# Two graph convolutions: the sums of all blocks kept in PSUM, one-hots made from SBUF operands

## The chip, the cores and the metric

The program runs on one NeuronCore of a Trainium2 chip, as one launch. The metric is the device time of that launch in microseconds (us). Before the change it is 5357.61 us, the median of three runs (5348.63 to 5358.73).

## The reference

The whole is a two-layer network over a graph of 6250 nodes (256 features) and 100,000 edges, sorted by destination. The change touches only the second layer's graph part and the mixing part that runs beside it. The graph part is two graph convolutions, one after the other:

```
h   = x @ W                                  # to 64 columns
msg = h[src] * (dinv[src] * dinv[dst])
agg = segment_sum(msg, dst) + h * dinv**2    # 6250 x 64
out = relu(agg + b)
```

The second one is computed as its sum first and its product with W2 (64 to 256 columns) afterwards, so both sum rows of 64 columns. The mixing part needs, over all nodes, the sum of `v^T k` per pair of 128 columns and the sum of `k` (k and v are layer-normalised per head of 32), and after that, for each node, `gelu(x_n @ M + c) @ w2 + b2 + x_n`.

## The kernel before

Nodes are cut into NB = 49 blocks of 128, edges into NT = 782 tiles of 128. Since the edges are sorted, a tile lies in one block or in a few neighbouring ones; each pair (tile, block) is a *step*. With the steps that are split at block borders and padding there are 832 steps, in NG = 104 groups of GS = 8. Tables made earlier on the chip say for each step which block it belongs to (`btab`), in which slot of a ring its tile lies (`stab`), and for each group how many groups of tiles must have landed (`need`).

`convolve(nc, m, a, which)` runs twice, for which = 0 and 1. Five engines work at once, each with its own program:

- GpSimd (L1850 to L1861) issues one indirect DMA for each tile (L1857): 128 rows of 64 floats, gathered from the table `t_d` in HBM by the row numbers in `m.srct` (SBUF), into one of 96 ring slots (12 groups). Ahead of a group g it waits until group g-2 has landed, and counts it in `tiles_in` (L1853, L1854); and it waits until the step groups that could still read the slots are summed (`summed` >= g-4, L1856). Its program is written out in full, it has no loop.
- VectorE makes for each step group eight one-hots of 128 x 128 (`one_hot`, L1924): is_equal between `iota`, a copy in PSUM made at the start (L1905), and the local destinations `m.dl` in SBUF.
- TensorE (`total`, L2073 to L2082) multiplies each one-hot with its tile's rows into 64 columns of PSUM bank 0 or 1.
- VectorE adds these 64 columns into the block's row of `m.agg` in SBUF (`add`, L1926 to L1936), one instruction for each step, each waiting for the one before (`added`). `m.agg` starts as a copy of the node's own table (L1906).
- Beside this, for which = 0, TensorE projects each block to keys and values (`project`, L2089), VectorE adds the bias (`add_bias`, L1965) and scales (`scale`, L1954, L1958), ACT squares, and `sum_kv` (L2099, L2101) accumulates the sums in banks 4 to 7. For which = 1 `up` (L2111), ACT's gelu (L2057) and `down` (L2120) run the mixing network in banks 2 and 3. SyncE loads the block of transposed rows that they need (`load`, L1894), after the one before is used (`mixed`).

The order on each engine is written out by `pipeline`: in iteration k VectorE does one_hot(2k), add(2k-1), variance(k-1), one_hot(2k+1), add(2k), scale(k-1), add_bias(k). TensorE does total(2k), sum_kv(k-2), project(k), total(2k+1). After 52 iterations `refresh` (L1993 to L2000) scales, adds the bias, clips and scales again, in seven chunks of seven blocks, and SyncE stores the new table. A stage ends with a barrier of all engines. The convolutions stand between `combine_and_project` and `finish_and_route1`. The scoring stage of the first layer (`score_edges`) is of the same kind: 832 indirect DMAs from GpSimd (L653) beside VectorE's L692, L700 and L705.

Of the kernel before, what the change touches and what calls it, by code (L numbers as in the profile page):

```python
# [1805 lines left out]
def convolve(nc, m, a, which):  # L1806
# [4 lines left out]
    with ExitStack() as ctx:  # L1811
# [5 lines left out]
        oh = sb("oh", [P, 2, GS, P])  # L1817
        xt = sb("xt", [P, D])
        bank = [ctx.enter_context(nc.psum_tensor(f"v{which}_bank{i}", [P, 512], F32)) for i in range(8)]
        s = {n: m.sem(f"v{which}_" + n) for n in "in0 in1 tiles_in oh_ready summed added started xt_in weights".split()}  # L1820
        landed = [s["in0"], s["in1"]]
        iota = bank[3 + which][:, 0:P]
        table = m.t_d.rearrange("b p n -> (b p) n")
        if which == 0:
# [5 lines left out]
            b1row = sb("b1row", [P, MH])  # L1830
            s.update({n: m.sem("v0_" + n) for n in ("chain centred kv_made kvb_ready squared summed16 var_ready std_ready rstd_ready "
                                                    "kn_ready kv_used scaled biased table stored sums_out").split()})
            mixed = s["kv_made"]
        else:
# [7 lines left out]
            t_ps, m2_ps = (bank[i][:, :].rearrange("p (c d) -> p c d", c=KC) for i in (5, 6))  # L1842
            s.update({n: m.sem("v1_" + n) for n in ("ht_made ht_ready out_made xn_ready xb_ready mixed res_ready "
                                                    "fold_in chain kvt t_made t_back m2_made folded").split()})
            mixed = s["ht_made"]

        with nc.Block() as block:
            @block.gpsimd
            def _(pool):
                for g in range(TG):  # L1850
                    if g >= 2:
                        pool.wait_ge(landed[g % 2], 16 * GS * (g // 2))
                        pool.sem_inc(s["tiles_in"], 1)  # L1853
                    if g + NB // GS + 2 > RING // GS:  # L1854
                        pool.wait_ge(s["summed"], g + NB // GS + 2 - RING // GS)
                    for t in range(g * GS, min((g + 1) * GS, NT)):  # L1856
                        nc.gpsimd.indirect_dma_start(rows[:, t % RING, :], None, table,  # L1857
                                                     bass.IndirectOffsetOnAxis(ap=m.srct[:, t:t + 1], axis=0)).then_inc(landed[g % 2], 16)
                for g in (TG - 2, TG - 1):
                    pool.wait_ge(landed[g % 2], 16 * (GS * (g // 2) + min(GS, NT - g * GS)))  # L1860
                    pool.sem_inc(s["tiles_in"], 1)  # L1861

            @block.sync
            def _(sp):
# [26 lines left out]
                def load(k, u, r):  # L1891
                    if at_least(k, 1):
                        sp.wait_ge(mixed, k)
                    sp.dma_start(xt[:, :], block_rows(m.xnt_d, k)).then_inc(s["xt_in"], 16)  # L1894
                pipeline(sp, NB, 1, (0, load))
                if which == 0:
                    for c in range(NB // 7):
                        sp.wait_ge(s["table"], c + 1)
                        sp.dma_start(m.t_d[7 * c:7 * c + 7].rearrange("b p n -> p b n"), m.table[:, 7 * c:7 * c + 7, :]).then_inc(s["stored"], 16)
                    sp.wait_ge(s["stored"], 16 * (NB // 7))  # L1900

            @block.vector
            def _(dve):
                V = nc.vector
                V.tensor_copy(iota, m.iota[:, :]).then_inc(s["started"], 1)  # L1905
                V.tensor_copy(m.agg[:, :, :], m.table[:, :, :]).then_inc(s["started"], 1)  # L1906
                dve.wait_ge(s["started"], 2)
# [13 lines left out]
                def one_hot(g, u):  # L1921
                    if at_least(g, 2):
                        dve.wait_ge(s["summed"], g - 1)
                    V.tensor_tensor(oh[:, u, :, :], iota.unsqueeze(1).to_broadcast([P, GS, P]),  # L1924
                                    m.dl[:, bass.ds(g * GS, GS)].unsqueeze(2).to_broadcast([P, GS, P]),
                                    ALU.is_equal).then_inc(s["oh_ready"], 1)  # L1926

                def add(g, u):
                    dve.wait_ge(s["summed"], g + 1)
                    blocks = blocks_of(nc, m, mybir.EngineType.DVE, g * GS, GS)  # L1930
                    for k in range(GS):
                        t = g * GS + k
                        if at_least(t, 1):
                            dve.wait_ge(s["added"], t)
                        V.tensor_tensor(of_block(m.agg, blocks[k]), of_block(m.agg, blocks[k]), bank[u][:, k * MH:(k + 1) * MH],  # L1935
                                        ALU.add).then_inc(s["added"], 1)  # L1936
# [24 lines left out]
                def add_bias(k, u, r):  # L1961
# [3 lines left out]
                    V.tensor_tensor(kvb[:, :, :, :].rearrange("p t h d -> p (t h d)"), bank[2][:, :],  # L1965
# [10 lines left out]
                def finish(k, u, r):  # L1976
                    dve.wait_ge(s["xb_ready"], k + 1)
                    dve.wait_ge(s["out_made"], k + 1)
                    V.tensor_tensor(xb[:, :], xb[:, :], bank[3][:, 0:D], ALU.add).then_inc(s["mixed"], 1)
# [5 lines left out]
                def refresh():  # L1985

                    dve.wait_ge(s["added"], NS)
                    part = lambda t, c: t[:, 7 * c:7 * c + 7, :]
                    dinv = lambda c: m.dinv[:, 7 * c:7 * c + 7].unsqueeze(2).to_broadcast([P, 7, MH])
                    n = NB // 7  # L1990
                    for c in range(n + 2):
                        if c < n:
                            V.tensor_tensor(part(m.agg, c), part(m.agg, c), dinv(c), ALU.mult).then_inc(s["scaled"], 1)  # L1993
                        if 0 <= c - 1 < n:
                            dve.wait_ge(s["scaled"], c)
                            V.tensor_tensor(part(m.agg, c - 1), part(m.agg, c - 1), b1row[:, :].unsqueeze(1).to_broadcast([P, 7, MH]),
# [6 lines left out]
                def fold():  # L2003
# [9 lines left out]
                    for q in range(KC):  # L2013
# [12 lines left out]
                    V.tensor_tensor(m.c2[:, :], b1[:, :], bank[7][:, 0:KC], ALU.add).then_inc(s["folded"], 1)  # L2026

                conv = ((0, lambda k, u, r: one_hot(2 * k, 0)), (1, lambda k, u, r: add(2 * k + 1, 1)),
                        (0, lambda k, u, r: one_hot(2 * k + 1, 1)), (0, lambda k, u, r: add(2 * k, 0)))
                if which == 0:  # L2030
                    pipeline(dve, NR, 1, conv[0], conv[1], (1, variance, NB), conv[2], conv[3], (1, scale, NB), (0, add_bias, NB))
                    refresh()
                else:
                    fold()
                    dve.wait_ge(s["weights"], 32)
                    pipeline(dve, NR, 1, conv[0], conv[1], (1, normalise, NB), conv[2], conv[3], (1, finish, NB))

            @block.scalar
            def _(act):
# [12 lines left out]
                def gelu(k, u, r):  # L2052
# [3 lines left out]
                    for q in range(KC):  # L2056
                        last = nc.scalar.activation(ht[:, q, :], bank[2][:, q * P:(q + 1) * P], ACT.Gelu, bias=m.c2[:, q:q + 1])  # L2057
                    last.then_inc(s["ht_ready"], 1)
                if which == 0:
                    pipeline(act, NB, 1, (1, root), (0, square))  # L2060
                    act.wait_ge(s["kv_used"], NB)
                    for q in range(KC):
                        nc.scalar.copy(m.gram[:, q, 0:P + 1], bank[4 + q][:, 0:P + 1]).then_inc(s["sums_out"], 1)
                        nc.scalar.copy(m.gram[:, q, P + 1:2 * P + 1], bank[6 + q][:, 0:P]).then_inc(s["sums_out"], 1)
                    act.wait_ge(s["sums_out"], 2 * KC)
                else:
                    act.wait_ge(s["folded"], 2)
                    pipeline(act, NB, 1, (0, gelu))

            @block.tensor  # L2070
            def _(pe):
                def total(g, u):
                    pe.wait_ge(s["oh_ready"], g + 1)  # L2073
                    if at_least(g, 2):
                        pe.wait_ge(s["added"], GS * (g - 1))
                    tiles = tiles_needed(nc, m, mybir.EngineType.PE, g)
                    at = slots_of(nc, m, mybir.EngineType.PE, g * GS, GS)
                    pe.wait_ge(s["tiles_in"], tiles)
                    for k in range(GS):
                        last = nc.tensor.matmul(bank[u][:, k * MH:(k + 1) * MH], oh[:, u, k, :], of_block(rows, at[k]),  # L2080
                                                start=True, stop=True)
                    last.then_inc(s["summed"], 1)  # L2082

                def project(k, u, r):
# [3 lines left out]
                    for q in range(KC):  # L2088
                        last = nc.tensor.matmul(bank[2][:, :], xt[:, q * P:(q + 1) * P],  # L2089
# [3 lines left out]
                def sum_kv(k, u, r):  # L2093
                    rows_ = LAST if isinstance(k, int) and k == NB - 1 else P
                    first, final = isinstance(k, int) and k == 0, isinstance(k, int) and k == NB - 1
# [640 lines left out]
```

## Time and profile before

| What | Value |
|---|---|
| Timed runs | 5357.61 us median (5348.63 to 5358.73) |
| Profiled execution, first to last instruction | 5935.3 us |
| Window of convolution 0 | 2878 to 4045 us, then its end to 4088 us |
| Window of convolution 1 | 4089 to 5280 us |
| Gathers (L1857), both convolutions | 1564, 1483.7 us busy, 949 ns each |
| GpSimd idle before them | 957.2 us |
| Adds (L1935) | 1664, 366.5 us busy |
| One-hots (L1924) | 208, 253.7 us busy, 1220 ns each |
| Matmuls of the steps (L2080) | 3328 rows, 716.2 us busy |
| Gathers of the scoring stage (L653) | 832, 859.8 us busy, 1033 ns each |

The profiled execution is another one than the timed ones, and no time of it is recorded other than its span. An fp32 matmul stands in the rows as two passes, each with its load of weights. A row names line, engine, operation, and the tiles as out<-in; 128x1024 is partitions x elements. "Idle before" is the time in which that engine did nothing ahead of such a row, and the name behind the arrow is what ended it. The releaser is inferred from a semaphore's number; numbers are used again by later stages, so a name can be that of an earlier stage. "issue" is time in which the engine waited for nothing that the profile shows. The table of times and the page are read together: first the length of a stage, then which engine's row of instructions fills it.

### The profile page before, as it was taken

To read this page: it belongs to the slowest core of one execution; us is meant where nothing else is said; L and a number is where in the kernel's file an instruction comes from. 1 tells how busy PE (TensorE), PEld (TensorE's weight loads), DVE (VectorE), ACT (ScalarE), POOL (GpSimd) and SP (SyncE) were. 2 spreads that over 40 slices of the span, in tenths; PEclk is the share of its full clock that TensorE was granted. 3 is DMA by queue.
4 is the path that set the end of the run, shared out by engine and by line. 5 is a ranking of instruction groups with operands and counts; after the bars stand their busy time and mean duration, and the time that the engine had idled before them with its cause. 6 is when DMAs were issued, how large, how long until landed. Compare 5 with 4: busy or idle time off the path is not lost. (4 is left out here: it accounts for less than half of the span.)

```text
span 5935.3 us, 66919 instructions
## 1 busy us (share of the span) xinstructions
PE 3546.3 (60%) x13782; PEld 2710.2 (46%) x13783; DVE 2982.8 (50%) x6982; ACT 1018.9 (17%) x2146; POOL 3055.9 (51%) x2888
## 2 busy tenths in 40 slices
PE   4744455454389865998444544454445454466998
PEld 3633233232267654776433433333434444455666
DVE  5466566666899964445433333334333333354443
ACT  0111121121179801221000000000000000013121
POOL 1266677676368624221466666663666666612111
PEclk9877767776599976998566566655555555566999
DMA  4487666666578762223311111111111111123221
GB/s 108 136 217 211 202 207 203 204 206 195 158 227 271 224 188 88 63 63 97 106 28 28 29 28 28 29 29 32 28 29 28 28 29 28 29 62 98 70 87 37
DMA packets 432122, 617.01 MB, mean 104 GB/s; under 512 B 100329, under 2 KB 309161, under 8 KB 431721
## 3 DMA queue, kind: packets, MB, share of 16 engines
q1 hardware_dynamic: 304733, 389.03, 21.1%
q0 software_dynamic: 107440, 200.97, 14.1%
q10 hardware_dynamic: 19852, 25.94, 1.6%
q8 instruction: 33, 0.54, 0.0%
q14 instruction: 64, 0.52, 0.0%
HBM read 419.67 MB, written 209.64 MB: 106 GB/s over the span
## 5 line engine op out<-in xcount | busy, mean ns | idle before, releaser
L1857 POOL DMA_INDIRECT big<-t_d,src_tiles x1564 | 1483.7, 949 | 957.2 <-issue 450.8
L2080 PE MATMUL v_bank<-big,v_oh 128*128 x3328 | 716.2, 390 | 1216.6 <-issue 830.3
L2080 PEld LDWEIGHTS v_bank<-big,v_oh 128*128 128x128 f32 x3328 | 674.7, 300 | 1302.8 <-issue 1302.2
L653 POOL DMA_INDIRECT big<-xl_d,src_steps x832 | 859.8, 1033 | 378.1 <-issue 356.0
L1935 DVE TENSOR_TENSOR big<-big,v_bank 128x64 f32 x1664 | 366.5, 220 | 1285.3 <-DMA xj_d<-big 973.2
L759 PE MATMUL se_z_ps<-big,se_oht 128*128 x1664 | 608.7, 517 | 628.5 <-issue 385.9
L759 PEld LDWEIGHTS se_z_ps<-big,se_oht 128*128 128x128 f32 x1664 | 386.8, 250 | 850.4 <-issue 780.7
L692 DVE TENSOR_TENSOR se_z<-se_z_ps,big 128x528 f32<-128x528 f32 x416 | 291.4, 700 | 461.1 <-DMA es_ts<-src_p 256.8
L1122 PE MATMUL ae_bank<-ae_v,ae_oh 128*128 128x266 f32 x1664 | 402.3, 397 | 49.8 <-DVE big L1106 36.7
L1081 POOL TENSOR_TENSOR ae_v<-ae_v,ex 128x1792 f32<-128x1792 f32 x104 | 334.1, 3215 | 178.1 <-DMA ae_v<-xj_d 178.0
L1122 PEld LDWEIGHTS ae_bank<-ae_v,ae_oh 128*128 128x128 f32 x1664 | 310.4, 191 | 141.5 <-DVE big L1106 53.0
L1106 DVE TENSOR_TENSOR big<-big,ae_bank 128x266 f32 x832 | 303.8, 425 | 13.2 <-PE ae_bank L1122 7.5
L1924 DVE TENSOR_TENSOR v_oh<-v_bank,dl_steps 128x1024 f32<-128x1024 f32 x208 | 253.7, 1220 | 92.5 <-issue 92.0
L729 ACT ACTIVATE se_oht<-se_dlb,se_place 128x1024 f32<-128x1024 bf16 x104 | 119.4, 1148 | 986.6 <-DMA es_ts<-src_p 498.3
L700 DVE SCALAR_TENSOR_TENSOR se_w<-se_z,se_attb 128x512 f32<-128x512 f32 x416 | 284.8, 685 | 0.1
L1599 POOL DMA_INDIRECT y_d<-e_y,e_idx x106 | 104.1, 982 | 348.1 <-DVE e_idx L1562 328.6
L705 DVE TENSOR_REDUCE ex<-se_w 128x512 f32 (+1 forms) x416 | 281.6, 677 | 0.0
L2526 POOL DMA_INDIRECT out<-e_y,e_idx x64 | 63.0, 984 | 422.3 <-DVE e_y L2569 407.6
L1069 ACT ACTIVATE ae_oh<-iota,dl_steps 128x128 f32<-128x128 f32 x832 | 254.5, 388 | 60.0 <-PE ae_bank L1122 51.7
L2622 PE MATMUL e_bank<-big,e_ht 128*128 128x256 f32 x1024 | 225.3, 381 | 0.7 <-issue 0.7
L2611 PE MATMUL e_bank<-e_xt,big 128*128 128x465 f32 (+1 forms) x512 | 214.4, 577 | 1.6 <-DVE e_xt L2545 1.6
L2057 ACT ACTIVATE v_ht<-v_bank,c 128x128 f32<-128x128 f32 x98 | 30.6, 363 | 1064.8 <-remote 780.8
(468 smaller groups left out, 5316.9 us busy)
## 6 DMA issues: line engine op xcount, KB each, us to landing
xj_d<-big SPq DMA_DIRECT2D x208, 528.0 KB
ae_v<-xj_d SPq DMA_DIRECT2D x208, 528.0 KB
se_dlb<-dlr_d SPq DMA_DIRECT2D x104, 256.0 KB
big<-t_d,src_tiles POOLq DMA_INDIRECT x1564
buf_d<-ne_blank SPq DMA_DIRECT2D x4, 4112.0 KB
e_xs<-buf_d SPq DMA_DIRECT2D x106, 129.0 KB, 2.1
big<-xl_d,src_steps POOLq DMA_INDIRECT x832
cp_y<-y_d SPq DMA_DIRECT2D x14, 896.0 KB, 7.4
```

The costliest lines, as they stand in the source:

```text
L653: nc.gpsimd.indirect_dma_start(half_of(u)[:, k, :], None, table, bass.IndirectOffsetOnAxis(ap=m.src[:, t:t + 1], axis=0)).then_inc(landed[ ...
L692: nc.vector.tensor_tensor(z[:, u, k:k + 2, :], z_ps[v % 4][:, :, 0:LW], xj[:, u, k:k + 2, :], ALU.add).then_inc(s["z_ready"], 1)
L700: nc.vector.scalar_tensor_tensor(w[:, v % 2, :, :], z[:, u, k:k + 2, 0:D], 0.0, wide, ALU.max, ALU.mult).then_inc(s["weighed"], 1)
L705: nc.vector.tensor_reduce(m.ex[:, bass.ds(q * 2 * H, 2 * H)], w[:, v % 2, :, :].rearrange("p k (h c) -> p (k h) c", h=H), AX.X, ALU.add)\
L759: last = nc.tensor.matmul(z_ps[v % 4][:, i, 0:LW], oht[:, u, k + i, :], of_block(m.xr, blocks[2 * (v % 2) + i]), start=True, stop=True)
L1069: nc.scalar.activation(oh[:, w % 2, k, :], m.iota[:, :], ACT.Abs, bias=m.dl[:, bass.ds(g * GS + k, 1)], scale=-1.0).then_inc(s["oh_apart"], 1)
L1081: nc.gpsimd.tensor_tensor(x, x, ex, ALU.mult).then_inc(s["high_ready"], 1)
L1106: V.tensor_tensor(to, to, bank[k][:, 0:AW], ALU.add).then_inc(s["added"], 1)
L1122: nc.tensor.matmul(bank[k][:, 0:AW], oh[:, w % 2, k, :], v[:, w, k, :], start=True, stop=True)\
L1857: nc.gpsimd.indirect_dma_start(rows[:, t % RING, :], None, table, bass.IndirectOffsetOnAxis(ap=m.srct[:, t:t + 1], axis=0)).then_inc(lande ...
L1935: V.tensor_tensor(of_block(m.agg, blocks[k]), of_block(m.agg, blocks[k]), bank[u][:, k * MH:(k + 1) * MH], ALU.add).then_inc(s["added"], 1)
L2080: last = nc.tensor.matmul(bank[u][:, k * MH:(k + 1) * MH], oh[:, u, k, :], of_block(rows, at[k]), start=True, stop=True)
```

## The change

- The sums of all 49 blocks stay in PSUM: seven banks of eight blocks (`sums`, 64 columns each). TensorE writes each step's product there directly, accumulating, at an address read from `btab`. `seed` puts the node's own table there first, with seven matmuls by the identity. `add` and its semaphore are gone, and so are the copies L1905 and L1906.
- The one-hots read `m.iota` in SBUF in place of the copy in PSUM, and stand in `m.ex`.
- The eighth bank (`side`) serves `project`, or `up` and `down`. The sums of `v^T k` and of `k` go into the free columns of the seventh bank of sums; the sum of `k` is made as one column instead of 128 equal rows and spread at the end by ACT and two matmuls.
- SyncE, in place of GpSimd, waits for the landed groups and counts them in `tiles_in`; each of its iterations counts two groups, waits for `mixed`, and issues the next load.
- In convolution 1 `down` of a block comes at the end of the same iteration as `up` (before: one iteration later), and at the end VectorE and ACT copy the sums to `m.agg`. `refresh` reads its first operand from PSUM, in chunks of eight blocks.

```diff
         NR = NG // 2
-        oh = sb("oh", [P, 2, GS, P])
+        PB = 512 // MH
+        NK = -(-NB // PB)
+        oh = m.ex[:, 0:2 * GS * P].rearrange("p (u k n) -> p u k n", u=2, k=GS)
-        bank = [ctx.enter_context(nc.psum_tensor(f"v{which}_bank{i}", [P, 512], F32)) for i in range(8)]
+        sums = ctx.enter_context(nc.psum_tensor(f"v{which}_sums", [P, NK, PB, MH], F32))
+        side = ctx.enter_context(nc.psum_tensor(f"v{which}_side", [P, 512], F32))
+        agg = sums[:, :, :, :].rearrange("p c b n -> p (c b) n")
-        iota = bank[3 + which][:, 0:P]
...
+            last = sums[:, NK - 1, :, :].rearrange("p b n -> p (b n)")
+            kv_ps = [last[:, MH + 136 * q:MH + 136 * q + P + 1] for q in range(KC)]
+            ksum_ps = last[:, MH + 136 * KC:MH + 136 * KC + KC]
...
                     if g >= 2:
                         pool.wait_ge(landed[g % 2], 16 * GS * (g // 2))
-                        pool.sem_inc(s["tiles_in"], 1)
...
-                def load(k, u, r):
-                    if at_least(k, 1):
-                        sp.wait_ge(mixed, k)
+                def load(k):
                     sp.dma_start(xt[:, :], block_rows(m.xnt_d, k)).then_inc(s["xt_in"], 16)
-                pipeline(sp, NB, 1, (0, load))
+                def tiles_landed(k, u, r):
+                    for i in range(2):
+                        sp.wait_ge(landed[i], 16 * GS * (k + 1))
+                        sp.sem_inc(s["tiles_in"], 1)
+                    sp.wait_ge(mixed, k + 1)
+                    load(k + 1)
+                load(0)
+                pipeline(sp, NB - 1, 1, (0, tiles_landed))
...
-                V.tensor_copy(iota, m.iota[:, :]).then_inc(s["started"], 1)
-                V.tensor_copy(m.agg[:, :, :], m.table[:, :, :]).then_inc(s["started"], 1)
-                dve.wait_ge(s["started"], 2)
...
-                    V.tensor_tensor(oh[:, u, :, :], iota.unsqueeze(1).to_broadcast([P, GS, P]),
+                    V.tensor_tensor(oh[:, u, :, :], m.iota[:, :].unsqueeze(1).to_broadcast([P, GS, P]),
                                     m.dl[:, bass.ds(g * GS, GS)].unsqueeze(2).to_broadcast([P, GS, P]),
                                     ALU.is_equal).then_inc(s["oh_ready"], 1)
-
-                def add(g, u):
-                    dve.wait_ge(s["summed"], g + 1)
-                    blocks = blocks_of(nc, m, mybir.EngineType.DVE, g * GS, GS)
-                    for k in range(GS):
...
-                        V.tensor_tensor(of_block(m.agg, blocks[k]), of_block(m.agg, blocks[k]), bank[u][:, k * MH:(k + 1) * MH],
-                                        ALU.add).then_inc(s["added"], 1)
...
+                    dve.wait_ge(s["summed"], NG)
+                    for c in range(NK // 2):
+                        V.tensor_copy(m.agg[:, PB * c:PB * c + PB, :], agg[:, PB * c:PB * c + PB, :]).then_inc(s["agg_out"], 1)
...
+                def seed():
+                    for c in range(NK):
+                        lo, hi = PB * c, min(PB * c + PB, NB)
+                        nc.tensor.matmul(agg[:, lo:hi, :].rearrange("p b n -> p (b n)"), m.ident[:, :],
+                                         m.table[:, lo:hi, :].rearrange("p b n -> p (b n)"), start=True, stop=True)
+
                 def total(g, u):
                     pe.wait_ge(s["oh_ready"], g + 1)
-                    if at_least(g, 2):
-                        pe.wait_ge(s["added"], GS * (g - 1))
                     tiles = tiles_needed(nc, m, mybir.EngineType.PE, g)
                     at = slots_of(nc, m, mybir.EngineType.PE, g * GS, GS)
+                    to = blocks_of(nc, m, mybir.EngineType.PE, g * GS, GS)
                     pe.wait_ge(s["tiles_in"], tiles)
                     for k in range(GS):
-                        last = nc.tensor.matmul(bank[u][:, k * MH:(k + 1) * MH], oh[:, u, k, :], of_block(rows, at[k]),
-                                                start=True, stop=True)
+                        last = nc.tensor.matmul(of_block(agg, to[k]), oh[:, u, k, :], of_block(rows, at[k]),
+                                                start=False, stop=True, skip_group_check=True)
                     last.then_inc(s["summed"], 1)
...
-                    pipeline(dve, NR, 1, conv[0], conv[1], (1, variance, NB), conv[2], conv[3], (1, scale, NB), (0, add_bias, NB))
+                    pipeline(dve, NR, 1, even, (1, variance, NB), odd, (1, scale, NB), (0, add_bias, NB))
...
-                    pipeline(pe, NR, 1, even, (1, down, NB), (0, up, NB), odd)
+                    seed()
+                    pipeline(pe, NR, 1, even, (0, up, NB), odd, (0, down, NB))
```

## Rows read from the trace of the kernel before

**Rows 1.** The page's first line.

```profile
span 5935.3 us, 66919 instructions
```

**Rows 2.** Groups of convolution 0's window: xcount | busy us, mean ns | idle before.

```profile
L1857 POOL DMA_INDIRECT big<-t_d,src_tiles x782 | 743.3, 951 | 489.2 <-issue 225.9 <-DMA xj_d<-big 163.5 <-POOLq L134 98.4
L2080 PE MATMUL v_bank<-big,v_oh 128*128 x1584 | 319.0, 375 | 621.5 <-issue 361.2 <-DVE big L1935 259.8
...
L1935 DVE TENSOR_TENSOR big<-big,v_bank 128x64 f32 x785 | 172.8, 220 | 559.8 <-DMA xj_d<-big 412.9 <-PE v_bank L2080 31.5 <-issue 19.7
L2089 PE MATMUL v_bank<-v_wkv,v_xt 128*128 128x512 f32 x196 | 146.7, 890 | 4.4 <-issue 4.2
L1924 DVE TENSOR_TENSOR v_oh<-v_bank,dl_steps 128x1024 f32<-128x1024 f32 x100 | 122.0, 1220 | 39.3 <-issue 39.2
```

**Rows 3.** The same for convolution 1's window.

```profile
L1857 POOL DMA_INDIRECT big<-t_d,src_tiles x782 | 740.3, 947 | 468.0 <-issue 224.9 <-DMA xj_d<-big 160.6 <-POOLq L134 76.4
L2080 PE MATMUL v_bank<-big,v_oh 128*128 x1664 | 379.1, 403 | 590.8 <-issue 464.8 <-DVE big L1935 116.1 <-DVE v_oh L1924 8.0
```

**Rows 4.** Timeline of GpSimd (start us, us, what, [idle before]), two first gathers.

```profile
3552.57 0.94 POOL L1857 DMA_INDIRECT big<-t_d,src_tiles  x1 [3.38 <-DMA xj_d<-big]
...
3563.58 0.94 POOL L1857 DMA_INDIRECT big<-t_d,src_tiles  x1 [1.33 <-DMA xj_d<-big]
```

**Rows 5.** Timeline, a projection on TensorE and the bias add that waits for it.

```profile
3531.01 2.22 PE L2089 MATMUL v_bank<-v_wkv,v_xt 128*128 128x512 f32 x4
...
3552.18 0.69 DVE L1965 TENSOR_TENSOR v_kvb<-v_bank,v_bkv 128x512 f32<-128x512 f32 x1 [1.03 <-DMA se_dlb<-dlr_d]
```

**Rows 6.** Timeline, GpSimd's last gather of convolution 0, and later adds.

```profile
4011.64 0.94 POOL L1857 DMA_INDIRECT big<-t_d,src_tiles  x1 [0.30 <-issue]
...
4055.75 2.76 DVE L1935 TENSOR_TENSOR big<-big,v_bank 128x64 f32 x8 [1.18 <-PE v_bank L2080]
...
4060.89 2.76 DVE L1935 TENSOR_TENSOR big<-big,v_bank 128x64 f32 x8 [1.24 <-PE v_bank L2080]
...
4070.78 2.76 DVE L1935 TENSOR_TENSOR big<-big,v_bank 128x64 f32 x8 [2.46 <-PE v_bank L2080]
```

**Rows 7.** Register loads by source line: ns min/median/max (L373 block numbers, L378 slots).

```profile
L373 DVEq TENSOR_LOAD <-tabs x312: 593/598/852, 1648.9 to 5275.0; - x156
...
L378 PEldq TENSOR_LOAD <-tabs x208: 585/590/715, 2894.4 to 5270.5; - x104
```

**Rows 8.** Groups of the scoring stage, 240 to 1520 us.

```profile
L653 POOL DMA_INDIRECT big<-xl_d,src_steps x832 | 859.8, 1033 | 378.1 <-issue 356.0 <-DVE se_z L692 20.6 <-DMA xj_d<-big 1.5
...
L700 DVE SCALAR_TENSOR_TENSOR se_w<-se_z,se_attb 128x512 f32<-128x512 f32 x416 | 284.8, 685 | 0.1
```

**Rows 9.** Timeline, the first work of each convolution.

```profile
2878.00 1.78 DVE L1906 COPY big<-big 128x3136 f32<-128x3136 f32 x1
2878.43 2.23 POOL L1857 DMA_INDIRECT big<-t_d,src_tiles  x1 [98.39 <-POOLq L134]
...
2895.19 3.67 PE L2080 MATMUL v_bank<-big,v_oh 128*128 x16 [21.73 <-issue]
...
4089.00 2.20 POOL L1857 DMA_INDIRECT big<-t_d,src_tiles  x1 [76.42 <-POOLq L134]
...
4119.06 3.67 PE L2080 MATMUL v_bank<-big,v_oh 128*128 x16 [7.98 <-DVE v_oh L1924]
```

**Rows 10.** Timeline of the scoring stage, VectorE's L700 beside gathers.

```profile
606.47 0.68 DVE L700 SCALAR_TENSOR_TENSOR se_w<-se_z,se_attb 128x512 f32<-128x512 f32 x1
606.61 1.37 POOL L653 DMA_INDIRECT big<-xl_d,src_steps  x1 [0.30 <-issue]
...
608.28 0.72 DVE L700 SCALAR_TENSOR_TENSOR se_w<-se_z,se_attb 128x512 f32<-128x512 f32 x1
608.28 0.95 POOL L653 DMA_INDIRECT big<-xl_d,src_steps  x1 [0.30 <-issue]
```

More of the change, by code:

```diff
@@ L1978, in finish @@
                     dve.wait_ge(s["out_made"], k + 1)
-                    V.tensor_tensor(xb[:, :], xb[:, :], bank[3][:, 0:D], ALU.add).then_inc(s["mixed"], 1)
+                    V.tensor_tensor(xb[:, :], xb[:, :], y_ps, ALU.add).then_inc(s["mixed"], 1)
                     dve.wait_ge(s["mixed"], k + 1)
@@ L2056, in gelu @@
                     for q in range(KC):
-                        last = nc.scalar.activation(ht[:, q, :], bank[2][:, q * P:(q + 1) * P], ACT.Gelu, bias=m.c2[:, q:q + 1])
+                        last = nc.scalar.activation(ht[:, q, :], h_ps[:, q * P:(q + 1) * P], ACT.Gelu, bias=m.c2[:, q:q + 1])
                     last.then_inc(s["ht_ready"], 1)
@@ L2061, in _ @@
                     act.wait_ge(s["kv_used"], NB)
+                    act.wait_ge(s["summed"], NG)
+                    nc.scalar.copy(ksum[:, :], ksum_ps).then_inc(s["sums_out"], 1)
                     for q in range(KC):
-                        nc.scalar.copy(m.gram[:, q, 0:P + 1], bank[4 + q][:, 0:P + 1]).then_inc(s["sums_out"], 1)
-                        nc.scalar.copy(m.gram[:, q, P + 1:2 * P + 1], bank[6 + q][:, 0:P]).then_inc(s["sums_out"], 1)
-                    act.wait_ge(s["sums_out"], 2 * KC)
+                        nc.scalar.copy(m.gram[:, q, 0:P + 1], kv_ps[q]).then_inc(s["sums_out"], 1)
+                    act.wait_ge(s["sums_out"], 1)
+                    for q in range(KC):
+                        nc.scalar.activation(kwide[:, q, :], m.iota[:, :], ACT.Identity, bias=ksum[:, q:q + 1], scale=0.0).then_inc(s["wide"], 1)
+                    act.wait_ge(s["spread"], 1)
+                    for q in range(KC):
+                        nc.scalar.copy(m.gram[:, q, P + 1:2 * P + 1], side[:, q * P:(q + 1) * P]).then_inc(s["sums_out"], 1)
+                    act.wait_ge(s["sums_out"], 2 * KC + 1)
                 else:
@@ L2088, in project @@
                     for q in range(KC):
-                        last = nc.tensor.matmul(bank[2][:, :], xt[:, q * P:(q + 1) * P],
+                        last = nc.tensor.matmul(side[:, :], xt[:, q * P:(q + 1) * P],
                                                 wkv[:, q, :, :, :].rearrange("p t h d -> p (t h d)"), start=(q == 0), stop=(q == KC - 1))
@@ L2116, in down @@
                     pe.wait_ge(s["ht_ready"], k + 1)
-                    if at_least(k, 1):
-                        pe.wait_ge(s["mixed"], k)
                     for q in range(KC):
-                        last = nc.tensor.matmul(bank[3][:, 0:D], ht[:, q, :], w2[:, q, :], start=(q == 0), stop=(q == KC - 1))
+                        last = nc.tensor.matmul(y_ps, ht[:, q, :], w2[:, q, :], start=(q == 0), stop=(q == KC - 1))
                     last.then_inc(s["out_made"], 1)
@@ L2124, in _ @@
                 if which == 0:
+                    seed()
                     pe.wait_ge(s["centred"], 1)
                     pipeline(pe, NR, 1, even, (2, sum_kv, NB), (0, project, NB), odd)
+                    pe.wait_ge(s["wide"], KC)
+                    for q in range(KC):
+                        last = nc.tensor.matmul(side[:, q * P:(q + 1) * P], kwide[:, q, :], m.ident[:, :], start=True, stop=True)
+                    last.then_inc(s["spread"], 1)
                 else:
```

77 lines of the change are left out of this document (42 added, 35 removed).

## The prediction

> **What bounds the kernel now.** I read the page first, then the groups of instructions in the windows of the two convolutions, then the timeline where GpSimd pauses, and last two places where VectorE and GpSimd are seen together. The page gives a span of 5935.3 us, and the program runs on one core [rows 1]. The two windows are 1167 and 1191 us long, 40% of the span. In each, GpSimd issues 782 gathers (L1857). They take 743.3 us plus 225.9 us of "issue" between them in the first window, so a gather costs 0.94 + 0.30 = 1.25 us and the row of 782 costs 977 us. On top of that come 163.5 and 160.6 us of waiting [rows 2, 3]. No other engine is near that: VectorE's adds (L1935) and one-hots (L1924) are 172.8 + 122.0 us, TensorE's L2080 is 319.0 us. So GpSimd's issue is the floor of both convolutions: 977 us each, and then the tail.
>
> What is the waiting? It is always ahead of the first gather of a group of 8: at 3552.57 after 3.38 us, at 3563.58 after 1.33 us [rows 4]. The releaser's name, an old DMA, is a leftover of a reused semaphore number; the gather's own wait in the code is the one on `summed` (slots of the ring come free). TensorE's rows of that time show project's four passes from 3531.01 on, for 2.22 us, but VectorE's `add_bias` (L1965), which waits for them alone, starts at 3552.18 only [rows 5]. So in the profiled execution TensorE's completions come up to 19 us behind its rows, and `summed` with them. When GpSimd has stopped (last gather at 4011.64 us) this is gone: the adds of two groups start at 4055.75 and 4060.89, 5.1 us apart [rows 6], far below the 10 us that GpSimd needs for 8 gathers.
>
> I take this lag to be mostly a thing of the profiled execution. The three timed runs have a median of 5357.6 us, 577.7 us below the profiled span, and that must come from somewhere. The waits that the lag makes are 163.5 + 160.6 = 324 us in the convolutions; at the end of each, some 62 us pass from the last gather to the last add (4011.64 to 4073.5), of which about 50 are backlog, 100 in both; and in the scoring stage the gathers' idle time is 378.1 us where 832 x 0.30 = 250 would do [rows 6, 8], 128 more. Together 552 of the 578 us. This is an inference, no row shows an unprofiled run; it is the step on which the sign hangs. By it the timed convolution is 977 us of gathers plus a short tail, with GpSimd never waiting.
>
> **The change, part by part.** The sum is made on the profiled rows and carried to the median, because the slack that would hide it in the profiled execution (324 us of GpSimd's waits) is taken to be missing there.
>
> *The adds go* (832 a convolution, 0.22 us each, and a load of block numbers of 0.60 us per group [rows 2, 7]). In the loop they lie beside the gathers and are worth nothing. In the tail the last group's load and adds stand before the end: 0.60 + 2.76 = 3.4 us [rows 6, 7], twice, -6.7 us. If the backlog of about 12 groups were there in the timed runs too, they would be worth more (first rival).
>
> *The start.* L1906 copies 3136 elements for 1.78 us from SBUF to SBUF, and the first gather beside it takes 2.23 us where a later one takes 0.94 [rows 4, 9]. Copy and delay go: -1.3 us, twice, -2.6 us. For it come seven identity matmuls (`seed`). TensorE's 512-column passes take 0.89 us, two a matmul [rows 2], 12 us in all. In convolution 0 they fit between the stage's start and TensorE's first work, 2878 to 2895.19, while the weights are centred. In convolution 1 they stand after the fold: TensorE's first group is at 4119.06, 30 us after the first gather, and would be at 4131; GpSimd may run five groups (50 us) ahead [rows 9]. Nothing. Without that cover it would be 12 us.
>
> *TensorE* loads the block numbers in VectorE's place, another 0.59 us per group [rows 7], and resolves a second register address per matmul. If TensorE were the bound, the loads would cost 208 x 0.59 = 123 us; a group's matmuls take 3.67 us [rows 9] and its gathers 10, so it is covered. `ksum` in one column instead of 128 is a small saving, covered too.
>
> *SyncE counts the tiles.* GpSimd loses one increment per group: nothing. SyncE's loop waits for both groups, then for `mixed`, then issues the next x^T load. Behind its wait stands only that load, needed an iteration (19 us) later, and the next count. The count of group 2k+2 waits for project(k) or up(k), which TensorE does before it needs that tile. 0, from 0 to 2 us.
>
> *The ends.* Convolution 0: the refresh reads the same 3136 elements, from PSUM; ACT's copies and the two spreading matmuls run beside its 11 us. 0 to +1. Convolution 1: sums must go to SBUF, three 512-element copies on VectorE at 0.69 (L1965 has this size from PSUM [rows 5]) beside four on ACT: +2.1 us.
>
> *The one-hots* are the term that decides. Today L1924 has iota in PSUM, takes 1.22 us, and gathers beside it stay at 0.94 us. With iota and `dl` both in SBUF I expect the same 1.2 us on VectorE, which has room. But in the scoring stage, L700 has both inputs in SBUF, and there the gathers' mean is 1033 ns where an undisturbed one takes 0.95 us [rows 8, 10]. Rows show how: the L700 that runs from 606.47 to 607.15 holds the gather that started at 606.61 until 607.98, 1.37 us, 0.83 after L700's end; one that starts together with a gather (608.28) costs it nothing [rows 10]. So a gather needs something by about 0.12 us after its start and waits for VectorE's end. A VectorE operation of length L that falls anywhere in the 1.25 us cycle then costs on average (L - 0.12)^2 / (2 x 1.25): 0.13 us for L = 0.685, 0.48 us for L = 1.22. Measured for L700: (1033 - 950) x 832 / 416 = 0.17 us. Scaling the measured value by the squares of L - 0.12 gives 0.63, by the lengths 0.30; I take 0.5. At least three one-hots a convolution come after the last gather, so 202 count: +101 us. The ends are 0 (never at a gather's start) and 1.1 x 202 = +222 us (always just before one). The phase is not random, since one-hots follow landings, and that is why both ends stay in the range.
>
> The trace shows that such an operation delays gathers. The Trainium skill, "SBUF — State Buffer", section "Who interferes with whom", says that a VectorE instruction with two SBUF inputs contends with a GpSimd instruction that reads SBUF, but also that the original probe saw `tensor_tensor` leave DMAs alone, as descriptor generation needs the write interface. By the second sentence the term would be 0 and the time that of the second rival; these gathers read their row numbers from SBUF, and by the first the term stands.
>
> Sum: +101 - 6.7 - 2.6 + 2.1 = +94 us, 5357.6 + 94 = 5452 us; I say 5450.
>
> **Rivals.**
>
> 1. *The lag is real in the timed runs.* Then GpSimd has its 324 us of slack there, which swallow the delays, and the removed adds count. For: the rows themselves. Against: the 578 us would have no place. In the tail, 12 groups that follow every 5.1 us would go at TensorE's own 3.7 us [rows 9]: 17 us a convolution, 34. In the loops, TensorE's idle time put down to the adds is 259.8 and 116.1 us [rows 2, 3]; in convolution 0 the next one-hot stands behind `add_bias` as before, so little goes; in convolution 1 I give half, 58. The longer loads take back some 35 (a quarter or so of their 123). -57: 5300 us. Faster.
>
> 2. *One-hots don't disturb gathers* (their phase misses the start, or `is_equal` with broadcast inputs isn't like L700). For: L700 cost its gathers nothing in more than half of the cases. Against: its mean. 101 us fall out: 5350 us, no change that can be told.
>
> 3. *They fall badly.* The one-hot is issued in step with landings and sits just before a gather's start nearly every time: 1.0 us x 202 = 202 us, 5553 us. For: nothing random sets the phase. Against: two one-hots an iteration come by different paths. It decides from about 0.9 us each.
>
> The forecast is slower; rivals 1 and 2 end on the other side.
>
> **How the numbers follow.** Forecast (0.2 to 0.85 us per one-hot, 5390 to 5522 us) 0.59, rival 1 0.20, rival 2 0.12, rival 3 0.09. Below 5310 lies about half of rival 1, above 5540 most of rival 3: 0.18 left out. About 0.2% (11 us) is what a measurement of this kernel tells from no change. Faster: rival 1 and a little of 2, 0.22. Same: most of rival 2, 0.09. Slower: 0.69.
>
> **What would show it.** Right: in the two windows the gathers' mean is about 1010 ns in place of 951 and 947 (0.5 x 101 / 782 = 65 ns more), with single gathers of 1.3 to 2.0 us, each ending 0.83 us after a one-hot; one-hots of 1.2 us; the first gather of each convolution at 0.94; no rows of adds; 2 us of copies at the end. GpSimd's waits at group starts, 324 us now, shrink in the profile, so the profiled span may move far less than the timed median, or even fall. Wrong: gathers at 0.95 beside one-hots (rival 2), or a timed median below 5330 (rival 1). A wait of SyncE's count that TensorE shows at L2080, or GpSimd's waits grown over 324 us, would show a step that I cost at nothing.

## The result

The kernel after takes 5448.2 us (median of 4 runs, 5437.0 to 5455.3), the kernel before 5357.5 in the same runs: ratio 1.0173, 95% interval 1.0158 to 1.0188, +91 us. The forecast was 5450, slower. But only some 75 us come by the predicted way, where +101 was put down, and another 20 to 30 come from a step that the prediction priced at nothing; small gains take some of it back.

The profile of the kernel after: span, then groups (xcount | busy us, mean ns | idle before). A q behind an engine's name (POOLq, SPq) means its queue of instructions.

```profile
span 5435.3 us, 63942 instructions
L1865 POOL DMA_INDIRECT big<-t_d,src_tiles x1564 | 1553.9, 994 | 630.0 <-issue 492.4
L2103 PE MATMUL v_sums<-big,ex 128*128 x3328 | 701.4, 398 | 585.6 <-SPq L1902 552.0
L653 POOL DMA_INDIRECT big<-xl_d,src_steps x832 | 831.8, 1000 | 253.9 <-issue 243.2
L2112 PE MATMUL v_side<-v_wkv,v_xt 128*128 128x512 f32 x196 | 175.6, 1049 | 144.9 <-DMA v_xt<-xnt_d 144.9
L1936 DVE TENSOR_TENSOR ex<-iota,dl_steps 128x1024 f32<-128x1024 f32 x208 | 254.5, 1224 | 839.1 <-PE v_sums L2103 839.1
L2133 PE MATMUL v_side<-v_xt,m 128*128 128x128 f32 x392 | 98.3, 431 | 191.7 <-DMA v_xt<-xnt_d 191.7
```

A gather (L1865) takes 994 ns in the mean, 951 and 947 before [rows 2, 3]. The profiled span lies within 2 us of the time of the same execution (5437.0), and GpSimd now sits idle for 253.9 us before L653, whose code did not change, and not for 378.1 [rows 8]. That points to the profile of before as the odd one. Two rows have no counterpart in what was expected: the projections L2112 and L2133 wait 144.9 and 191.7 us for their own load.

### The profile page after: what moved, and what is told of

It reads as the page before. It is cut to its first block and busy times, and to the rows that moved or that the text cites. A ratio compares the mean times of both kernels' runs of the same rounds, so it can differ in the third digit from the quotient of the medians.

```text
span 5435.3 us, 63942 instructions
## 1 busy us (share of the span) xinstructions
PE 3566.8 (66%) x13814; PEld 2745.7 (51%) x13815; DVE 2634.4 (48%) x5317; ACT 1021.7 (19%) x2153; POOL 3098.6 (57%) x2888
## 3 DMA queue, kind: packets, MB, share of 16 engines
q1 hardware_dynamic: 304733, 389.03, 22.5%
## 5 line engine op out<-in xcount | busy, mean ns | idle before, releaser
L1865 POOL DMA_INDIRECT big<-t_d,src_tiles x1564 | 1553.9, 994 | 630.0 <-issue 492.4
L2103 PE MATMUL v_sums<-big,ex 128*128 x3328 | 701.4, 398 | 585.6 <-SPq L1902 552.0
L2103 PEld LDWEIGHTS v_sums<-big,ex 128*128 128x128 f32 x3328 | 681.5, 308 | 686.9 <-issue 683.9
L653 POOL DMA_INDIRECT big<-xl_d,src_steps x832 | 831.8, 1000 | 253.9 <-issue 243.2
L759 PE MATMUL se_z_ps<-big,se_oht 128*128 x1664 | 634.5, 548 | 449.2 <-issue 392.0
L759 PEld LDWEIGHTS se_z_ps<-big,se_oht 128*128 128x128 f32 x1664 | 429.2, 272 | 654.5 <-issue 562.9
L1936 DVE TENSOR_TENSOR ex<-iota,dl_steps 128x1024 f32<-128x1024 f32 x208 | 254.5, 1224 | 839.1 <-PE v_sums L2103 839.1
L700 DVE SCALAR_TENSOR_TENSOR se_w<-se_z,se_attb 128x512 f32<-128x512 f32 x416 | 285.9, 687 | 0.1
L2112 PE MATMUL v_side<-v_wkv,v_xt 128*128 128x512 f32 x196 | 175.6, 1049 | 144.9 <-DMA v_xt<-xnt_d 144.9
L2133 PE MATMUL v_side<-v_xt,m 128*128 128x128 f32 x392 | 98.3, 431 | 191.7 <-DMA v_xt<-xnt_d 191.7
L1953 DVE RECIPROCAL v_rstd<-v_std 128x16 f32<-128x16 f32 x49 | 12.4, 253 | 436.6 <-PE v_sums L2123 436.6
```

The costliest lines, as they stand in the source:

```text
L653: nc.gpsimd.indirect_dma_start(half_of(u)[:, k, :], None, table, bass.IndirectOffsetOnAxis(ap=m.src[:, t:t + 1], axis=0)).then_inc(landed[ ...
L700: nc.vector.scalar_tensor_tensor(w[:, v % 2, :, :], z[:, u, k:k + 2, 0:D], 0.0, wide, ALU.max, ALU.mult).then_inc(s["weighed"], 1)
L759: last = nc.tensor.matmul(z_ps[v % 4][:, i, 0:LW], oht[:, u, k + i, :], of_block(m.xr, blocks[2 * (v % 2) + i]), start=True, stop=True)
L2103: last = nc.tensor.matmul(of_block(agg, to[k]), oh[:, u, k, :], of_block(rows, at[k]), start=False, stop=True, skip_group_check=True)
```

## Experiment 1: the kernel before, profiled once more

> The kernel before, unchanged, profiled once more. My reading of the first profile: TensorE's completions, late by up to 19 us behind its rows, were a thing of that one execution, and the timed runs don't have them. Expected by that: a span near 5350 us, no waits of some 10 us before the first gather of a group in the convolutions, tails like those of the kernel after, and a mean gather of about 0.945 us with 0.30 us between two, so that 782 gathers take about 980 us. If the waits belong to the kernel (rival 1), the span is again above 5800 us and the waits stand where they stood.

Measured: 5351.0 us, span 5349.2. Its page:

```profile
span 5349.2 us, 66919 instructions
L1857 POOL DMA_INDIRECT big<-t_d,src_tiles x1564 | 1480.3, 947 | 622.9 <-issue 461.4
L2080 PE MATMUL v_bank<-big,v_oh 128*128 x3328 | 683.7, 391 | 917.1 <-POOLq L1853 858.3
L653 POOL DMA_INDIRECT big<-xl_d,src_steps x832 | 833.4, 1002 | 253.9 <-issue 240.8
L1924 DVE TENSOR_TENSOR v_oh<-v_bank,dl_steps 128x1024 f32<-128x1024 f32 x208 | 253.4, 1219 | 2.2
```

TensorE now waits for tiles (POOLq, 858.3 us), and GpSimd no longer waits for TensorE (0.3 us in all): the lag belonged to the one execution, as the prediction took it, and rival 1 falls. This profile is the one to compare with. Stretches, from the start of the first gather of each convolution to the start of its last one (us):

| | first gather | gathers 0 | between | gathers 1 | last gather to end |
|---|---|---|---|---|---|
| before (experiment 1) | 2685.1 | 987.9 | 27.8 | 988.5 | 659.8 |
| after | 2683.9 | 1028.1 | 36.0 | 1019.8 | 667.4 |
| difference | -1.2 | +40.2 | +8.2 | +31.3 | +7.6 |

71.5 us lie among the gathers, 15.8 behind their ends, where a gain of some 5 was forecast (-6.7 + 2.1).

In the kernel after, the projections wait 336.6 us for their load, where L2089 and L2111 of experiment 1 waited for nothing, and the sums (L2103) sit idle 331.5 us less than L2080. The waiting has moved from the sums to the projections. TensorE's granted clock (0.72 of full speed in the mean after, 0.74 before) doesn't explain the time: experiment 2 ran at the clock of before (0.736 to 0.741) and was still 87 us slower.

## Where the 71.5 us go

Timeline of the kernel after, VectorE's one-hots (L1936) and the gathers beside them:

```profile
3000.32 0.94 POOL L1865 DMA_INDIRECT big<-t_d,src_tiles  x1 [0.30 <-issue]
3001.32 1.22 DVE L1936 TENSOR_TENSOR ex<-iota,dl_steps 128x1024 f32<-128x1024 f32 x1
3001.57 1.78 POOL L1865 DMA_INDIRECT big<-t_d,src_tiles  x1 [0.30 <-issue]
...
3005.54 1.22 DVE L1936 TENSOR_TENSOR ex<-iota,dl_steps 128x1024 f32<-128x1024 f32 x1 [2.12 <-PE v_sums L2103]
3006.15 1.43 POOL L1865 DMA_INDIRECT big<-t_d,src_tiles  x1 [0.30 <-issue]
```

The same in the profile of experiment 1, where the one-hot reads one operand from PSUM:

```profile
3009.83 0.95 POOL L1857 DMA_INDIRECT big<-t_d,src_tiles  x1 [0.30 <-issue]
3010.14 1.21 DVE L1924 TENSOR_TENSOR v_oh<-v_bank,dl_steps 128x1024 f32<-128x1024 f32 x1
3011.08 0.94 POOL L1857 DMA_INDIRECT big<-t_d,src_tiles  x1 [0.30 <-issue]
```

The one-hot from 3001.32 ends at 3002.54; the gather beside it ends 0.81 later, at 3003.35. The one that ends at 3006.76 has its gather end at 3007.58, 0.82 later. Below it, the gather from 3011.08 started under a one-hot that still had 0.27 us to run, and took 0.94. Over all rows of the kernel after, 172 of the 202 one-hots between the first and last gathers are followed at 0.82 us by the end of a late gather, 69.8 us together, 0.35 each. A one-hot that begins up to 0.1 us after a gather's start (15 of them) holds nothing up. The residual's add (L1984, both operands in SBUF too, and 0.43 us long) does the same as the one-hots in 43 of 49 blocks, 6.8 us. In experiment 1, 192 one-hots stood over the point 0.12 us after a gather's start, and not one of these gathers was late.

## Experiment 2: the operand alone

```diff
-V.tensor_tensor(oh[:, u, :, :], iota.unsqueeze(1)...
+V.tensor_tensor(oh[:, u, :, :], m.iota[:, :].unsqueeze(1)...   # kernel before
```

> The kernel before with one edit: the one-hots read the row of column numbers from SBUF, where it is kept anyway, not from the PSUM bank. PSUM banks, adds, and the counting of tiles stay as they were. Theory (a one-hot whose operands both lie in SBUF holds up the gather that starts under it): 206 such one-hots at the 0.34 us that the profile of the kernel after gives for each, +70 us, so about 5428 us, the mean gather up from about 0.945 to about 0.99 us. Rival (the time of the kernel after comes from the sums in PSUM, the matmuls addressed by a register or the counting on SyncE): 5358 us and gathers as before.

Measured: 5439.3 us, ratio 1.0159 (1.0142 to 1.0176), +87 us. Its groups:

```profile
L1857 POOL DMA_INDIRECT big<-t_d,src_tiles x1564 | 1563.5, 1000 | 621.0 <-issue 466.5 <-POOLq L134 125.6 <-DMA big<-t_d,src_tiles 28.9
L1924 DVE TENSOR_TENSOR v_oh<-iota,dl_steps 128x1024 f32<-128x1024 f32 x208 | 253.6, 1220 | 2.2
```

VectorE's own time is the same (1220 ns); the gathers' mean rises from 947 to 1000. 160 of 206 one-hots hold a gather up, 78.3 us together, 0.38 for each of the 206. That is more than the 70 expected from the kernel after, since they fall elsewhere in the gathers' cycle. This one operand, moved alone, costs nearly what the whole change costs. It does not follow that the rest costs nothing: in the kernel after, with the second cost (below) taken out, the same operand costs some 61 us (run 5).

## Experiments 3, 4 and 10: other makers, shorter pieces

Experiment 3, on the kernel after, takes `one_hot` from VectorE:

```diff
+for k in range(GS):
+    nc.scalar.activation(oh[:, u, k, :], m.iota[:, :], ACT.Abs, bias=m.dl[:, bass.ds(g * GS + k, 1)], scale=-1.0)
+nc.scalar.activation(oh[:, u, :, :], oh[:, u, :, :], ACT.Relu, bias=m.ones[:, 0:1], scale=-1.0)
```

> The kernel after with its one-hots made on ScalarE, which is nearly idle in the convolutions: eight instructions of |row - destination| and one of max(1 - x, 0) for a group of eight steps, some 4 us of ScalarE in each group's 10 us. VectorE keeps the rest of its work. Theory: the 70 us of delayed gathers go, about 5375 us, gathers at about 0.945 us but for a few under the residual's add. Whatever stays above 5357 is the price of the other edits (I can't place 12 to 20 us of the 91 yet). Rival (the other edits cost the time): 5448 us, gathers at about 0.99 us only if they are not the cause.

Measured: 5385.7 us, 1.0055 (1.0038 to 1.0071). Its gathers:

```profile
L1865 POOL DMA_INDIRECT big<-t_d,src_tiles x1564 | 1482.8, 948 | 636.8 <-issue 495.5
```

Delays are down from 78.8 to 5.5 us in all and the gathers back to 948 ns, -73 us; yet the time falls by 62 only. From the last gather to the last sum (the tail) it is now 26.2 and 22.5 us where the kernel after has 20.4 and 16.6, since ScalarE takes 3.6 us for a one-hot where VectorE takes 1.2, and the last five groups queue for it. That, and the 33 us still missing to before, pointed to the tails.

Experiments 4 and 10 cut each one-hot in two and in four:

```diff
+for h in range(2):      # experiment 10: range(4), two steps each
+    last = V.tensor_tensor(oh[:, u, 4 * h:4 * h + 4, :], m.iota[:, :]..., m.dl[:, bass.ds(g * GS + 4 * h, 4)]..., ALU.is_equal)
```

> The kernel after with each one-hot as two instructions of four steps, one right behind the other. If a gather waits at its start for the end of the VectorE instruction that is under way, the wait is shorter with shorter instructions: by (L - 0.12)^2 / (2 x 1.25) for each, 0.12 us for L = 0.67 against 0.48 for L = 1.22, half the delay for two, so about 35 us off 5448: 5413 us. If the gather isn't let in between two instructions that follow within 0.1 us, or if the delay goes by the number of elements (a share of the ports), the time stays at 5448 us.

> The kernel after with each one-hot as four instructions of two steps. The whole one cost 69.8 us of delays and 5448 us, the halves 46.8 us and 5418 us. If a gather's wait at its start ends with the VectorE instruction under way, four of about 0.37 us cost (0.37 - 0.12)^2 / 2.5 = 0.025 us each, 21 us in all: 5395 to 5400 us. If instructions back to back act as one, the delays fall no further than the halves': 5418 us.

Measured: 5418.4 us (1.0116, 1.0099 to 1.0133) and 5393.0 us (1.0070, 1.0055 to 1.0085). The groups of experiment 10:

```profile
L1865 POOL DMA_INDIRECT big<-t_d,src_tiles x1564 | 1501.6, 960 | 631.4 <-issue 492.3
L1937 DVE TENSOR_TENSOR ex<-iota,dl_steps 128x256 f32<-128x256 f32 x832 | 298.1, 420 | 795.6 <-PE v_sums L2105 795.6
```

The delays by one-hots: 69.8 whole, 46.8 in halves, 19.6 in quarters. So a gather gets in between two instructions back to back, and waits only for the one under way. The law (L - 0.12)^2 / (2 x 1.25) gives 39 to 53 us for the halves and 15 to 30 for the quarters, by whether L is the distance from one piece to the next (0.61 and 0.34 us) or the length of its row (0.69 and 0.42), as the rows overlap. The measured 46.8 and 19.6 lie inside. For the whole one-hot it gives 100, which is too much: that one starts 0.2 to 0.6 us after a gather's start in more than half of the cases, and so ends soon after the next one's start.

## Experiments 5, 6 and 7: the second cost

The end of convolution 0 in the kernel after:

```profile
3712.06 0.94 POOL L1865 DMA_INDIRECT big<-t_d,src_tiles  x1 [0.30 <-issue]
...
3716.61 3.65 PE L2103 MATMUL v_sums<-big,ex 128*128 x16 [1.13 <-issue]
...
3721.74 10.76 PE L2103 MATMUL v_sums<-big,ex 128*128 x48
...
3732.53 1.29 DVE L1997 TENSOR_TENSOR big<-v_sums,dinv 128x512 f32<-128x512 f32 x2 [5.88 <-PE v_sums L2103]
...
3748.07 0.94 POOL L1865 DMA_INDIRECT big<-t_d,src_tiles  x1 [35.06 <-POOLq L134]
```

and in the kernel before (experiment 1):

```profile
3673.06 0.94 POOL L1857 DMA_INDIRECT big<-t_d,src_tiles  x1 [0.30 <-issue]
...
3678.16 3.67 PE L2080 MATMUL v_bank<-big,v_oh 128*128 x16 [2.81 <-DVE big L1935]
...
3682.62 2.76 DVE L1935 TENSOR_TENSOR big<-big,v_bank 128x64 f32 x8 [3.34 <-PE v_bank L2080]
...
3700.84 2.20 POOL L1857 DMA_INDIRECT big<-t_d,src_tiles  x1 [26.83 <-POOLq L134]
```

A group of eight steps is 16 rows of matmuls. After the last gather has started, TensorE of the kernel before begins one more group; that of the kernel after begins four, with one under way. SyncE's waits during the gathers of convolution 0 say why, first after, then before:

```profile
SPq L1902 <- DMA big<-t_d,src_tiles: 960.8, 96, 12.2
SPq L1897 <- PE v_side L2112: 2.2, 1, 2.2
```

```profile
SPq L1894 <- PE v_bank L2089: 877.4, 48, 23.3
```

Before, the load of the next block's nodes (L1894) waits for the projection alone. Now SyncE first counts both tile groups of the round (L1902), and only then issues the load. There are 832 steps for 782 tiles, so a group of steps needs an ever earlier group of tiles: in experiment 1 the first matmul of group 90 comes when 698 gathers have begun, in the kernel after at 713, because the projection ahead of it waits for a load that waits for tiles it doesn't need. Up to group 57 of 104 the two kernels are within 6 gathers of each other; from there the distance grows to 29.

> The kernel after with GpSimd counting landed tiles again and SyncE issuing each load of a block's nodes as soon as the last one is used, as before. New theory for the rest of the 91 us (second cost): in the kernel after SyncE issues the load for round k only after it has counted tile groups 2k-2 and 2k-1. TensorE's steps need ever fewer tiles as block boundaries are padded (in the kernel before it ends up to 36 tiles, four to five groups, behind the gathers and loses nothing), so from the middle of a convolution the projection waits for its load, TensorE is held level with the gathers, and after the last gather five groups of steps are left: 20.4 and 16.6 us from the last gather to the last sum, 8.8 and 8.5 us before. Expected: 20 us off 5448, so 5428 us, tails near 9 us, no idle before the projection for its load (144.9 us in convolution 0 now); the delays of gathers stay. If the tail comes from the sums in PSUM or the reading of block numbers by TensorE: 5448 us.

> The kernel after, SyncE still counts tiles, but the loads of a block's nodes are issued from ScalarE's queue as soon as the last one is used. If it is the order (load behind count) that costs: as the run in which GpSimd counts, 5428 us and tails near 9 us. If it is that SyncE counts at all (its semaphore reaches TensorE later): only that other run gains and this one stays at 5448 us.

> The kernel before with one edit: SyncE counts landed tiles as in the kernel after, with the load of a block's nodes issued behind the two counts. One-hots, banks and adds as before. Second cost: tails from 8.8 and 8.5 us to some 20 and 17, or more since VectorE's adds stand in each group of the catching up: +20 to +30 us, 5375 to 5385 us. Without a second cost: 5353 us.

The edits, in their core:

```diff
# 5, on the kernel after: GpSimd counts, SyncE only loads
+pool.sem_inc(s["tiles_in"], 1)
-pipeline(sp, NB - 1, 1, (0, tiles_landed))
+pipeline(sp, NB, 1, (0, load))
# 6, on the kernel after: SyncE counts, ScalarE's queue loads
-sp.wait_ge(mixed, k + 1)
-load(k + 1)
+act.wait_ge(mixed, k + 1)
+nc.scalar.dma_start(xt[:, :], block_rows(m.xnt_d, k + 1)).then_inc(s["xt_in"], 16)
# 7, on the kernel before: the reverse of 5
```

Measured: 5: 5417.4 us, 1.0111 (1.0096 to 1.0126). 6: 5419.7 us, 1.0120 (1.0104 to 1.0135). 7: 5385.0 us, 1.0057 (1.0042 to 1.0073), +29. The projection's group in 5, then in 7:

```profile
L2107 PE MATMUL v_side<-v_wkv,v_xt 128*128 128x512 f32 x196 | 169.9, 1019 | 0.0
```

```profile
L2094 PE MATMUL v_bank<-v_wkv,v_xt 128*128 128x512 f32 x196 | 158.0, 953 | 145.7 <-DMA v_xt<-xnt_d 145.7
```

Tails (last gather to last sum): 7.2 and 7.1 us in 5; 7.6 and 7.1 in 6; 24.3 and 23.2 in 7, from 8.8 and 8.5 before. Since 5 and 6 agree, it is the place of the load behind the counts that costs; that SyncE counts costs nothing. Run 7 alone gives 30 us of longer tails for 29 us of time. Against the kernel after, run 5 is 31 us faster by the medians, 10 more than expected, with some 10 us of doubt either way. In the two profiles the tails are 22.7 us shorter. The one-hots' delays are 9.6 us less (60.2), since they fall elsewhere in the gathers' cycle, but the gathers' stretches are only 3.1 us shorter together, and what the 31 us have beyond these terms isn't placed.

## Experiments 8 and 9: both costs out

> Both costs taken out of the kernel after: one-hots on ScalarE, and GpSimd counts tiles. From the run with ScalarE alone (5386 us, tails 26.2 and 22.5 us) the tails should fall to about 9 us each, -31 us: 5355 us, level with the kernel before (5353) or a few us below it, for the sums that stay in PSUM save VectorE's last adds and the copies ahead of the first gather. If something else in the change costs time, it shows as what is left above 5353.

> The kernel after with GpSimd counting, and each one-hot written by VectorE in eight instructions that compare the one row of column numbers (one tensor from SBUF) with one number per partition, where the kernel after compares two tensors from SBUF in one instruction. Theory A (only an instruction that reads two tensors from SBUF holds a gather up): of the 62 us that the one-hots cost in conv 0 and 1 with GpSimd counting (5417 us) nothing stays, about 5350 us, gathers at 0.945 us. Theory B (any VectorE instruction that works from and to SBUF only holds it up, but each for its own short time, some 0.2 us): by (L - 0.12)^2 / (2 x 1.25) and L = 0.2, under 0.01 us each, 1664 of them, so 5350 to 5360 us too, but with some 100 gathers late by 0.05 to 0.1 us. Theory C (VectorE's load of the shared side counts, not the form, and eight instructions back to back act as one of 1.3 to 1.6 us): 5417 us or more.

```diff
# 9, with the counting of run 5; 8 joins runs 3 and 5
+for k in range(GS):
+    last = V.tensor_scalar(oh[:, u, k, :], m.iota[:, :], m.dl[:, bass.ds(g * GS + k, 1)], None, ALU.is_equal)
```

Measured: 8: 5356.6 us, 1.0001 (0.9992 to 1.0010). 9: 5365.8 us, 1.0013 (1.0004 to 1.0023). The gathers of 8, then the groups of 9:

```profile
L1866 POOL DMA_INDIRECT big<-t_d,src_tiles x1564 | 1486.3, 950 | 619.3 <-issue 451.0
```

```profile
L1866 POOL DMA_INDIRECT big<-t_d,src_tiles x1564 | 1496.5, 957 | 617.2 <-issue 453.1 <-POOLq L134 120.2 <-DMA big<-t_d,src_tiles 43.6
L1932 DVE TENSOR_SCALAR ex<-iota,dl_steps 128x128 f32<-128x128 f32 x1664 | 358.3, 304 | 801.8 <-PE v_sums L2098 801.4
```

In run 8, with both costs out, nothing of the 91 us is left, and nothing is gained: the sums in PSUM free VectorE, which was not the bound. Two small things cancel there. Behind the last gathers 5.7 us are saved against experiment 1, near the forecast, and other VectorE instructions (L1964, L1944) fall on gathers' starts: 10.5 us of delays where experiment 1 has 4.7. In run 9, 111 small instructions make a gather late, by 0.07 us each, 8.3 us: theory B's picture, at a price a little above what it gave. A shorter instruction helps, and its form need not have two tensors: these have one tensor and one number per partition from SBUF. The Trainium skill, "SBUF — State Buffer", section "Who interferes with whom", has both cases, the second input and the two-port modes that `tensor_scalar` can enter. The rows of run 9 agree that `tensor_scalar` can hold a gather up (the gathers' mean is 957 ns where 944 is undisturbed), but it does so in about half of the cases: some 200 gathers had one under way at their start. In experiment 1 a longer `tensor_scalar` (L1971) was under way at 24 starts with 2 late gathers. What decides was not tested. The same section says that `tensor_reduce` never contends on this chip, and the rows agree: in experiment 1, VectorE's reduce L1940 stood over the start of 31 gathers, none of them late. L1974, with two tensors from SBUF, stood over 8, and 7 were late:

```profile
L1940 DVE TENSOR_REDUCE v_var<-v_sq 128x16 f32<-128x512 f32 x49 | 33.2, 677 | 0.0
```

No run here beats the kernel before.

## Why the prediction was right, and where not

- *The bound and the lag.* Right: GpSimd's 1.25 us per gather is the floor (987.9 us in experiment 1, 977 predicted; the difference is mostly the pauses below), and the profiled lag was of that execution. The step on which the sign hung held.
- *The one-hots.* The mechanism was right to the detail (start, 0.12 us, end 0.82 us later), and of the two sentences that the prediction weighed, experiment 2 bears out the one on two SBUF inputs: these `tensor_tensor` do hold up indirect DMAs. The term was mis-sized: 0.5 x 202 = +101 was put down, 0.35 x 202 = 70 was measured; the gathers' mean is 994 ns, not 1010. The phase isn't random. And the price that was scaled up, 0.17 us for an L700, came from the odd profile: experiment 1 has 1002 ns for L653 where 1033 stood, which gives 0.10, and by the squares of L - 0.12 some 0.4. Missed beside it: L1984, +6.8 us.
- *"SyncE counts the tiles ... 0, from 0 to 2 us."* This step failed. The prediction saw that the load stands behind the count, and called it "needed an iteration (19 us) later". It is the next thing TensorE needs in that round, and what the round's steps need is older than what is counted: the kernel before starts a group of steps up to 29 gathers earlier. The price is +23 us by the tails of run 5 and +30 by those of run 7, and +28 to +33 by the medians of runs 5, 6 and 7, where 0 was written. It showed as idle time ahead of the projection, not at L2080, where the prediction had said to look.
- *Starts and ends.* First gather at 0.94 us, as said. With the order mended (run 5), 22.8 us lie between the two convolutions against 27.8: -5.0, where -3.4 was forecast (the -1.3 of each start falls among the gathers). At the end of convolution 1 run 5 stands at 664.5 us against 659.8, run 8 at 657.4, so the other stages' scatter hides a term of 1.3 us.
- *Seed, TensorE's loads, ksum.* Nothing that shows: run 8 leaves 0.6 us of median, though it is a sum of small terms of both signs, and these three were not tried one by one.

So 5450 came out because the one-hot term was some 24 us too large (101 against 69.8 + 6.8) and the order term 23 us too small in the tails alone. The sign and the main cause were right; the agreement to 2 us is luck.

## What to carry to other kernels

Where GpSimd issues indirect DMAs without a break, look for every VectorE instruction that reads two operands from SBUF: it can cost the bound engine time though VectorE's own row shows nothing. The sign is the gathers' mean, 994 ns where 944 is undisturbed. Leave one operand in PSUM, or cut the instruction into pieces; don't price it by VectorE's time. When a queue gets a second duty, ask for each instruction behind the new wait which round of the consumer needs it and which data that round really needs: a wait that is level with the fast producer holds back a consumer that was allowed to be ahead of it, and the bill comes after the last item. And compare the profiled span with the timed median before reading any wait.

## What the runs showed of the hardware

GpSimd pauses some 2.0 us, not 0.30, after gather 113 and then after every 112 more, six times in each convolution (the last row is one), in the kernel before as well. At 1.7 us more than usual each, that is some 10 us a convolution, most of what 987.9 has above 977. Its cause was not tested.

```profile
2832.04 0.94 POOL L1865 DMA_INDIRECT big<-t_d,src_tiles  x1 [0.30 <-issue]
2835.00 0.94 POOL L1865 DMA_INDIRECT big<-t_d,src_tiles  x1 [2.02 <-issue]
```

Left open: the row of column numbers kept in PSUM under the new bank plan. Every bank takes matmuls during the loop, and VectorE would read a bank that TensorE writes; what that costs, no run shows.
